# Context attention on one core: four of thirteen tiles squared on GpSimd, an addition in PSUM, and new cyclic orders for four engines

## The chip, the cores and the metric

The program runs on one core of a Trainium2 chip. Its time is the device time of the whole program in microseconds (us), from the launch to the last result in memory. A core has five engines that run their own instruction streams at the same time and wait for each other through semaphores: TensorE (PE in the profile; PEld is its loading of weights), VectorE (DVE), ScalarE (ACT), GpSimd (POOL) and SyncE (SP), which here issues the transfers. Matrix products land in PSUM, everything else lives in SBUF.

## The reference, cut to what matters

The program is a small Perceiver: six stages, of which the first and the fourth are the same kind of attention over a context of 1601 rows for each of 16 batches. The change is in that kind alone.

```python
y_dca, y_main = y[:, -16:, :], y[:, :-16, :]        # 1585 main rows of 256
q  = _ln((x @ Wq + bq).reshape(b, s1, 16, 32), qn_w, qn_b)
kv = concat([y_main @ Wk + bk, y_main @ Wv + bv])   # 512 columns each
k  = _ln(kv[..., :32], kn_w, kn_b)                  # normalised over each head's 32 columns
v  = kv[..., 32:]
ctx = softmax(q @ k.T * 32**-0.5) @ v               # 16 heads, 64 queries per batch
...
x = x + xattn_0(...); x = x + attn_0(...); x = x + ffn_0(...)
x = x + xattn_1(...); x = x + attn_1(...); x = x + ffn_1(...)
```

## The kernel before

`context_attention` is called twice in a run. It works through the 16 batches one after the other, and each batch's 1585 context rows in 13 tiles: twelve of 128 rows and a last one of 49. Values are held as the sum of a float16 part and a float16 rest, so that most products come in three matmuls.

For each tile i of the next batch: PE projects K (`k`, six matmuls of 512 columns into `ps_k`) and V (`v`, into `ps_v`); DVE takes K out of PSUM (`kc`), ACT squares it (`sq`, line 367, with a scale), DVE sums the squares of each head (`rd`, line 460); for each pair of tiles ACT makes a first guess of the inverse root (`r`, lines 373 and 377) and POOL refines it with five small instructions, one Newton step (`nw`, lines 300 to 310); ACT copies the root beside K (`rp`), DVE multiplies (`hat`), ACT and DVE write the float16 part and its rest (`kh`, `kl`), and SP transposes the tile by a transfer. V is split likewise by ACT (`vh`, line 400) and DVE (`vl`, line 482). The context itself is split chunk by chunk by ACT (`yh`) and POOL (`yl`). PE also makes first scores (`m`), of which DVE takes a maximum (line 493), needed to shift the queries (`tb`, `t`, `qs`, `qh`, `ql`; `qm` on POOL).

For the current batch there are 14 units of two tiles, seven for each half of the heads: PE makes the scores (`s`, line 650, into the one PSUM buffer `ps_t`), ACT takes the exponential twice (`e`, line 420 in float32 and 422 in float16), POOL subtracts the two to get the rest (`lo`, line 335), PE multiplies both with V and adds into `ps_o` (`pv`, line 677). After a half, DVE divides (`o`, lines 524 to 531) and the next half may overwrite `ps_o`.

`ps_k`, `ps_v`, `ps_h` and `ps_t` have one buffer each. So `s` of a unit waits until both exponentials of the unit before are done, `k` waits for `kc` of the tile before, and `v` for `vl` of the tile before.

No scheduler decides the order. `ORDER` is a table of four cyclic lists, one each for PE, ACT, DVE and POOL. One trip through a list is called a turn here; in each turn every step of one batch is done once on that engine. A trailing minus shifts a step by one batch back: in turn t, `k2-` is tile 2 of one batch and `s8--` unit 8 of the batch two before it in the pipeline. `batches` walks each list from two turns ahead of the first batch to two behind the last, and leaves out what no batch asks for. Each engine runs its list in order, so an instruction that waits holds up all that stands behind it on that engine. The last batch's `s` and `pv` stand outside the lists. SP has its own fixed loop, which the change doesn't touch.

Of the kernel before, what the change touches and what calls it, by code (L numbers as in the profile page):

```python
# [40 lines left out]
PER = KT // CHUNKS  # L41
WIDEST = MAIN - (CHUNKS - 1) * PER * P + 1
# [10 lines left out]
    PE: k2- pv6-- m7-- s8-- v0- k3- pv7-- s9-- m8-- pv8-- v1- k4- s10-- m9-- v2- pv9-- m10-- s11-- k5- m11--
    PE: v3- s12-- m12-- pv10-- v4- tb-- k6- s13-- v5- k7- pv11-- v6- k8- s0- pv12-- pv13-- k9- v7- s1- m0-
    PE: k10- pv0- s2- m1- v8- k11- m2- s3- pv1-
    ACT: e5-- rp10-- vh11-- sq0- kh10-- e6-- rp11-- r6-- vh12-- yh1- kh11-- e7-- rp12-- sq1- e8-- kh12-- sq2-
    ACT: vh0- r0- sq3- e9-- rp0- vh1- kh0- e10-- vh2- rp1- r1- sq4- e11-- yh2- vh3- kh1- sq5- e12-- rp2- vh4-
    ACT: r2- kh2- qh-- sq6- rp3- vh5- yh3- kh3- e13-- rp4- sq7- vh6- kh4- r3- sq8- rp5- e0- kh5- vh7- rp6- e1-
    ACT: sq9- kh6- e2- vh8- sq10- rp7- yh0 r4- kh7- e3- rp8- vh9- sq11- kh8- e4- rp9- vh10- sq12- r5- kh9-
    DVE: kl10-- m5-- hat11-- kc1- rd0- m6-- kl11-- vl12-- kc2- hat12-- rd1- o0-- m7-- kc3- vl0- m8-- kl12--  # L60
    DVE: rd2- hat0- vl1- rd3- m9-- kl0- kc4- m10-- vl2- hat1- m11-- kc5- vl3- m12-- kl1- t-- rd4- rd5- hat2-
    DVE: qs-- vl4- kc6- kl2- ql-- hat3- vl5- kc7- kl3- rd6- hat4- rd7- kc8- kl4- vl6- hat5- o1-- kc9- kl5-
    DVE: rd8- vl7- hat6- m0- kc10- rd9- m1- kl6- vl8- hat7- rd10- kc11- kl7- m2- hat8- vl9- kc12- kl8- m3-
    DVE: rd11- hat9- vl10- m4- kl9- kc0 hat10- vl11- rd12-
    POOL: lo8-- nw0- lo9-- nw1- lo10-- yl2- lo11-- nw2- lo12-- yl3- qm- lo13-- nw3- lo0- lo1- lo2- nw4- yl0
    POOL: lo3- lo4- nw5- lo5- lo6- nw6- yl1 lo7-
# [3286 lines left out]
```

## Time and profile before

| | us |
|---|---|
| median of 3 runs | 3083.88 (3082.59 to 3091.93) |
| the profiled execution, whole | 3080.41 |
| its span (first to last instruction) | 3078.6 |
| PE busy | 2816.6 (91%) |
| DVE busy | 2570.9 (84%) |
| ACT busy | 2272.8 (74%) |
| POOL busy | 1615.3 (52%) |

Busy time is the union of an engine's instructions. PE's matmuls overlap: one starts before the one ahead of it has left, so for PE the distance between two starts says more than a duration. The two calls of the context attention cover about 104 to 1084 us and 1773 to 2753 us of the span; the rest is self attention, the expert layer and the last layer.

### The profile page before, as it was taken

What the parts mean: (1) busy time and instruction counts of PE and PEld (TensorE: products, weight loads), DVE (VectorE), ACT (ScalarE), POOL (GpSimd) and SP (SyncE); (2) the same over time, 40 slices, a digit from 0 to 9 for tenths busy, and PEclk for the clock granted to TensorE, in tenths of its full rate; (3) what the DMA queues carried; (4) which work ended last, traced back from release to release, by engine and by line L of the source; (5) the groups of instructions that cost most, each with busy time, mean ns of one, the idle gap of its engine ahead of it and who ended that gap; (6) DMA issues with size and microseconds to landing.
All of it is one profiled execution on the core that took longest, in us unless ns stands there. A gap on an engine that the chain in (4) does not pass through costs nothing. (4 is left out here: it accounts for less than half of the span.)

```text
span 3078.6 us, 94131 instructions
## 1 busy us (share of the span) xinstructions
PE 2816.6 (91%) x37417; PEld 1666.0 (54%) x37417; DVE 2570.9 (84%) x4146; ACT 2272.8 (74%) x4155; POOL 1615.3 (52%) x2006
## 2 busy tenths in 40 slices
PE   7689999999999778789996779999999999968889
PEld 3245555555555556577773325555555555545646
DVE  6699999999999656768875679999999999957752
ACT  6479999999999854446664458999999999964431
POOL 1257777777777643212223326777777777752200
PEclk9899999999999889899998899999999999979989
DMA  3345554555554244349895345545555555430020
GB/s 126 95 87 87 97 84 89 94 87 86 94 89 82 56 158 151 133 167 299 301 304 150 104 85 94 90 86 92 90 85 94 88 87 93 73 93 1 1 75 28
DMA packets 542717, 328.93 MB, mean 107 GB/s; under 512 B 459381, under 2 KB 504565, under 8 KB 536522
## 3 DMA queue, kind: packets, MB, share of 16 engines
q1 hardware_dynamic: 534314, 295.63, 43.2%
q0 software_dynamic: 7680, 25.17, 2.8%
q8 instruction: 301, 4.93, 0.7%
q10 hardware_dynamic: 288, 2.10, 0.2%
q14 instruction: 134, 1.10, 0.1%
HBM read 181.86 MB, written 36.09 MB: 71 GB/s over the span
## 5 line engine op out<-in xcount | busy, mean ns | idle before, releaser
L335 POOL TENSOR_TENSOR a_elo<-a_e 128x1024 f16<-128x1024 f32 x428 | 856.5, 2001 | 285.6 <-ACT a_e L422 285.6
L590 PE MATMUL a_ps_k<-l_wk,a_yh 128*128 128x512 f16 (+1 forms) x1664 | 571.3, 384 | 32.5 <-POOL a_yl L317 22.0
L590 PE MATMUL a_ps_v<-l_wv,a_yh 128*128 128x512 f16 (+1 forms) x1664 | 567.8, 382 | 17.9 <-DVE a_v L482 16.9
L493 DVE TENSOR_REDUCE a_mx<-a_ps_m 128x2 f32<-128x1024 f32 x384 | 467.7, 1218 | 20.3 <-PE a_ps_m L616 20.0
L420 ACT ACTIVATE a_e<-a_ps_t 128x1024 f32<-128x1024 f32 x428 | 409.3, 956 | 42.4 <-PE a_ps_t L650 39.9
L422 ACT ACTIVATE a_e<-a_ps_t 128x1024 f16<-128x1024 f32 x428 | 410.5, 959 | 0.0
L650 PE MATMUL a_ps_t<-a_qb,a_kk 64*128 64x128 f16 (+1 forms) x9672 | 351.0, 219 | 8.9 <-ACT a_e L422 8.3
L650 PEld LDWEIGHTS a_ps_t<-a_qb,a_kk 64*128 64x128 f16 (+1 forms) x9672 | 281.6, 96 | 122.8 <-issue 90.7
L590 PE MATMUL a_ps_k<-l_wk,a_yl 128*128 128x512 f16 (+1 forms) x832 | 318.4, 383 | 0.0
L452 DVE SCALAR_TENSOR_TENSOR a_kc<-a_ps_k,l_bk 128x512 f32<-128x512 f32 (+1 forms) x416 | 283.2, 681 | 41.4 <-PE a_ps_k L590 40.2
L590 PE MATMUL a_ps_v<-l_wv,a_yl 128*128 128x512 f16 (+1 forms) x832 | 315.9, 380 | 0.0
L400 ACT ACTIVATE a_v<-a_ps_v 128x512 f16<-128x512 f32 (+1 forms) x416 | 255.4, 614 | 73.0 <-PE a_ps_v L590 60.3
L590 PEld LDWEIGHTS a_ps_k<-l_wk,a_yh 128*128 128x128 f16 (+1 forms) x1664 | 164.1, 99 | 255.0 <-issue 63.1
L677 PEld LDWEIGHTS a_ps_o<-a_v,a_e 128*64 128x64 f16 (+1 forms) x6480 | 230.0, 113 | 131.5 <-issue 98.8
L482 DVE SCALAR_TENSOR_TENSOR a_v<-a_ps_v,a_v 128x512 f16<-128x512 f32 (+1 forms) x416 | 284.3, 683 | 15.7 <-ACT a_v L400 11.2
L392 ACT ACTIVATE a_khl<-a_ps_h,a_one 128x512 f16<-128x512 f32 (+1 forms) x416 | 284.1, 683 | 16.4 <-DVE a_ps_h L467 15.9
L467 DVE TENSOR_TENSOR a_ps_h<-a_kc,a_ps_h 128x512 f32<-128x512 f32 (+1 forms) x416 | 285.8, 687 | 9.6 <-ACT a_ps_h L384 4.7
L590 PEld LDWEIGHTS a_ps_v<-l_wv,a_yh 128*128 128x128 f16 (+1 forms) x1664 | 163.1, 98 | 239.8 <-issue 43.3
L677 PE MATMUL a_ps_o<-a_v,a_e 128*64 128x65 f16 (+1 forms) x6480 | 273.4, 201 | 20.6 <-POOL a_elo L335 14.0
L475 DVE SCALAR_TENSOR_TENSOR a_khl<-a_ps_h,a_khl 128x512 f16<-128x512 f32 (+1 forms) x416 | 283.0, 680 | 1.7 <-ACT a_khl L392 1.7
L367 ACT ACTIVATE a_sq<-a_kc 128x512 f32<-128x512 f32 (+1 forms) x416 | 260.2, 625 | 26.0 <-DVE a_kc L452 23.4
L460 DVE TENSOR_REDUCE a_var<-a_sq 128x16 f32<-128x512 f32 (+1 forms) x416 | 277.8, 674 | 0.0
(415 smaller groups left out, 5283.9 us busy)
## 6 DMA issues: line engine op xcount, KB each, us to landing
l_land<-in_ctx SPq DMA_DIRECT2D x96, 384.0 KB, 3.9
l_ob<-in_m_w SPq DMA_DIRECT2D x32, 1024.0 KB, 8.0
f_w<-in_m_w SPq DMA_DIRECT2D x32, 512.0 KB, 4.8
...
```

What stands on the lines that cost most here:

```text
L335: pool.tensor_tensor(rest[0:r, :, 0:w], full[0:r, :, 0:w], high[0:r, :, 0:w], ALU.subtract)\
L392: act.activation(khl[0:r, n % 2, 0, :], ps_h[0:r, :], ACT.Identity, bias=one[0:r, 0:1])\
L420: act.activation(full[0:r, :, 0:w], src[0:r, :, 0:w], ACT.Exp)
L422: act.activation(high[0:r, :, 0:w], src[0:r, :, 0:w], ACT.Exp).then_inc(e_done, 1)
L452: dve.scalar_tensor_tensor(out=kc[0:r, kc_slot(at, i), :], in0=ps_k[0:r, :], scalar=1.0 / WSCALE, in1=bk[0:r, :], op0=ALU.mult, op1=ALU.ad ...
L467: dve.tensor_tensor(ps_h[0:r, :].rearrange("p (h d) -> p h d", d=HD), kc[0:r, kc_slot(at, i), :].rearrange("p (h d) -> p h d", d=HD), ps_h ...
L475: dve.scalar_tensor_tensor(out=khl[0:r, n % 2, 1, :], in0=ps_h[0:r, :], scalar=1.0, in1=khl[0:r, n % 2, 0, :], op0=ALU.add, op1=ALU.subtract)\
L482: dve.scalar_tensor_tensor(out=v[0:r, at.nbp, i, :, VLO:OW], in0=ps_v[0:r, :].rearrange("p (h d) -> p h d", d=HD), scalar=1.0 / WSCALE, in ...
L493: dve.tensor_reduce(mx[:, g, :, c], ps_m[:, :, :], AX.X, ALU.max).then_inc(mx_done, 1)
L590: m = pe.matmul(out[0:r, :], part[:, n % 2, c, cols], w[:, wpart, c, :], start=(c == 0 and a == 0), stop=(c == KC - 1 and a == 2))
L650: t = pe.matmul(dst[0:rows(i), r, col:col + P], kk[d, at.bp, kpart + g, k], qb[d, at.bp, g, qpart, :, :].rearrange("p a q -> p (a q)"), st ...
L677: t = pe.matmul(ps_o[q, a * OW:a * OW + w], part[k, r, col + 64 * par:col + 64 * par + 64], v[k, at.bp, i, 2 * pair + par, 0:w], start=fir ...
```

## The change

Four things change, all inside `context_attention`:

1. The squares of tiles 2, 5, 8 and 11 are taken by POOL, as a product of `kc` with itself, and no longer by ACT. DVE's sum waits on a new semaphore for them.
2. The square has no scale any more; the factor 1/32 is applied where the variance is read, in ACT's logarithm and in POOL's first Newton instruction, which adds the small constant in the same instruction (a product and a sum with two constants in place of a sum of two tensors).
3. In `out`, the sum of the two value parts is written back into `ps_o` in PSUM and no longer into `ob` in SBUF; the last product reads it there.
4. All four lists are in a new order. Their first step is another one too, so that the shifts (the minus signs) differ.

```diff
--- before.py
+++ after.py
@@ -39,6 +39,7 @@
 VLO = 33
 CHUNKS = 4
 PER = KT // CHUNKS
+POOL_SQUARES = (2, 5, 8, 11)
 WIDEST = MAIN - (CHUNKS - 1) * PER * P + 1
 WSCALE = 32.0
 LN_EPS, HEAD_EPS = 1e-5, 1e-6
@@ -49,21 +50,22 @@
 
 
 ORDER = """
-    PE: pv2-- v9-- k12-- s4-- m3-- v10-- pv3-- s5-- m4-- k0- v11-- pv4-- m5-- s6-- k1- v12-- s7-- pv5-- m6--
...
+    PE: m6-- s8-- k2- pv7-- s9-- m7-- k3- v1- pv8-- m8-- s10-- v2- m9-- k4- pv9-- s11-- m10-- v3- k5- m11--
...
 """
 
 
@@ -140,7 +142,7 @@
         q_in = [sem("q_in0"), sem("q_in1")]
         yh_done, yl_done = sem("yh_done"), sem("yl_done")
         k_done, v_done = sem("k_done"), sem("v_done")
-        kc_done, sq_done, red_done = sem("kc_done"), sem("sq_done"), sem("red_done")
+        kc_done, sq_done, red_done, psq_done = sem("kc_done"), sem("sq_done"), sem("red_done"), sem("psq_done")
         ln_done, r0_done, hat_done = sem("ln_done"), sem("r0_done"), sem("hat_done")
         newton = [sem(f"newton{j}") for j in range(5)]
         kh_done, kl_done, rp_done = sem("kh_done"), sem("kl_done"), sem("rp_done")
@@ -182,6 +184,10 @@
                 n = len(range(k, tiles, 2))
                 if n:
                     eng.wait_ge(turned[k], 16 * n)
+
+        def squared(tiles):
+            b, i = divmod(tiles, KT)
+            return b * len(POOL_SQUARES) + sum(k < i for k in POOL_SQUARES)
 
         def tiles_of(j):
             tp = j % TPAIRS
@@ -297,8 +303,7 @@
                     n, u, nt, r = at.nb * TPAIRS + p, (at.nbp * TPAIRS + p) % 2, len(tiles_of(p)), rows(2 * p)
                     v2, r2, a2, b2 = (t[0:r, u, 0:nt, :] for t in (var, r0, na, nb_))
                     pool.wait_ge(r0_done, n + 1)
-                    pool.tensor_tensor(a2, v2, eps[0:r, 0:nt * H].rearrange("p (t h) -> p t h", h=H), ALU.add)\
-                        .then_inc(newton[0], 1)
+                    pool.tensor_scalar(a2, v2, 1.0 / HD, HEAD_EPS, ALU.mult, ALU.add).then_inc(newton[0], 1)
                     pool.tensor_tensor(b2, r2, r2, ALU.mult).then_inc(newton[1], 1)
                     pool.wait_ge(newton[0], n + 1)
                     pool.wait_ge(newton[1], n + 1)
@@ -317,6 +322,13 @@
                     pool.tensor_tensor(yl[:, n % 2, :, 0:hi - lo], y[:, :, lo:hi], yh[:, n % 2, :, 0:hi - lo],
                                        ALU.subtract).then_inc(yl_done, 1)
 
+                def square(at, i):
+                    n, t, r = at.nb * KT + i, tile_par(at.nbp, i), rows(i)
+                    pool.wait_ge(kc_done, n + 1)
+                    need(pool, red_done, n - 1)
+                    full = kc[0:r, kc_slot(at, i), :]
+                    pool.tensor_tensor(sq[0:r, t, :], full, full, ALU.mult).then_inc(psq_done, 1)
+
                 def q_first(at):
 
                     pool.wait_ge(q_in[at.nbp], at.load)
@@ -340,6 +352,8 @@
                         newton_step(at, i)
                     elif kind == "yl":
                         y_low(at, i)
+                    elif kind == "sq" and i in POOL_SQUARES:
+                        square(at, i)
                     elif kind == "qm":
                         q_first(at)
                     elif kind == "lo" and (at.b < B - 1 or i % 2 == 0):
@@ -364,13 +378,14 @@
                     n, t, r = at.nb * KT + i, tile_par(at.nbp, i), rows(i)
                     act.wait_ge(kc_done, n + 1)
                     need(act, red_done, n - 1)
-                    act.activation(sq[0:r, t, :], kc[0:r, kc_slot(at, i), :], ACT.Square, scale=SCALE).then_inc(sq_done, 1)
+                    act.activation(sq[0:r, t, :], kc[0:r, kc_slot(at, i), :], ACT.Square).then_inc(sq_done, 1)
 
                 def guess(at, p):
 
                     n, u, nt, r = at.nb * TPAIRS + p, (at.nbp * TPAIRS + p) % 2, len(tiles_of(p)), rows(2 * p)
                     act.wait_ge(red_done, at.nb * KT + 2 * p + nt)
-                    act.activation(lnv[0:r, u, 0:nt, :], var[0:r, u, 0:nt, :], ACT.Ln, bias=eps[0:r, 0:1])\
+                    act.activation(lnv[0:r, u, 0:nt, :], var[0:r, u, 0:nt, :], ACT.Ln, scale=1.0 / HD,
+                                   bias=eps[0:r, 0:1])\
                         .then_inc(ln_done, 1)
                     need(act, newton[4], n - 1)
                     act.wait_ge(ln_done, n + 1)
@@ -424,7 +439,7 @@
                 def step(kind, i, at):
                     if kind == "yh":
                         y_high(at, i)
-                    elif kind == "sq":
+                    elif kind == "sq" and i not in POOL_SQUARES:
                         square(at, i)
                     elif kind == "r":
                         guess(at, i)
@@ -454,7 +469,10 @@
 
                 def variance(at, i):
                     n, t, r = at.nb * KT + i, tile_par(at.nbp, i), rows(i)
-                    dve.wait_ge(sq_done, n + 1)
+                    if i in POOL_SQUARES:
+                        dve.wait_ge(psq_done, squared(n + 1))
+                    else:
+                        dve.wait_ge(sq_done, n + 1 - squared(n + 1))
                     p = i // 2
                     need(dve, newton[4], at.nb * TPAIRS + p - 1)
                     dve.tensor_reduce(var[0:r, (at.nbp * TPAIRS + p) % 2, i % 2, :], sq[0:r, t, :].rearrange("p (h d) -> p h d", d=HD), AX.X, ALU.add)\
@@ -525,10 +543,10 @@
                     osum = ob[:, at.b, half * P:half * P + P].rearrange("p (a d) -> p a d", d=HD)
                     dve.tensor_copy(osum, o3[:, :, VLO:OW]).then_inc(os_done, 1)
                     dve.wait_ge(os_done, 2 * n + 1)
-                    dve.tensor_tensor(osum, o3[:, :, 0:HD], osum, ALU.add).then_inc(os_done, 1)
+                    dve.tensor_tensor(o3[:, :, 0:HD], o3[:, :, 0:HD], osum, ALU.add).then_inc(os_done, 1)
                     dve.wait_ge(rl_done, n + 1)
                     dve.wait_ge(os_done, 2 * n + 2)
-                    dve.tensor_tensor(osum, osum, rl[:, half, :].unsqueeze(2).broadcast_to([P, 4, HD]), ALU.mult)\
+                    dve.tensor_tensor(osum, o3[:, :, 0:HD], rl[:, half, :].unsqueeze(2).broadcast_to([P, 4, HD]), ALU.mult)\
                        .then_inc(o_done, 1)
 
                 def low(at, j):
```

The first place is PE's list around the units 7 to 9. `a_ps_t` are scores (128x128 x24 is a whole unit), `a_ps_m` first scores, `a_ps_k` and `a_ps_v` projections, `a_ps_o` the values. Before, from `s8` to the start of `pv7` (batches in the middle of the first call):

```order
L616 MATMUL a_ps_m<-a_kk,a_qm 128x512 x2
L650 MATMUL a_ps_t<-a_qb,a_kk 128x128 x24
L590 MATMUL a_ps_v<-l_wv,a_yh 128x512
L590 MATMUL a_ps_v<-l_wv,a_yl 128x512
L590 MATMUL a_ps_v<-l_wv,a_yh 128x512 x2
L590 MATMUL a_ps_v<-l_wv,a_yl 128x512
L590 MATMUL a_ps_v<-l_wv,a_yh 128x512
L590 MATMUL a_ps_k<-l_wk,a_yh 128x512
L590 MATMUL a_ps_k<-l_wk,a_yl 128x512
```

And after:

```order
L634 MATMUL a_ps_m<-a_kk,a_qm 128x512 x2
L668 MATMUL a_ps_t<-a_qb,a_kk 128x128 x24
L608 MATMUL a_ps_k<-l_wk,a_yh 128x512
L608 MATMUL a_ps_k<-l_wk,a_yl 128x512
L608 MATMUL a_ps_k<-l_wk,a_yh 128x512 x2
L608 MATMUL a_ps_k<-l_wk,a_yl 128x512
L608 MATMUL a_ps_k<-l_wk,a_yh 128x512
L695 MATMUL a_ps_o<-a_v,a_e 64x65 x2
```

Between `s8` and `pv7` (and so `s9`, which stands behind `pv7` in both) there were two projections, and now there is one.

The second place is ACT's list around the same units: `a_v` of 49 rows is `vh12`, `a_yh` is `yh1`, `a_khl` is `kh`, `a_e` are the exponentials, `a_ps_h` is `rp`. Before:

```order
L373 ACTIVATE a_lnv<-a_var,a_eps 49x16
L377 ACTIVATE a_r<-a_lnv 49x16
L400 ACTIVATE a_v<-a_ps_v 49x16x32
L361 ACTIVATE a_yh<-l_land 128x2x384
L392 ACTIVATE a_khl<-a_ps_h,a_one 128x512
L420 ACTIVATE a_e<-a_ps_t 128x1024
L422 ACTIVATE a_e<-a_ps_t 128x1024
L384 ACTIVATE a_ps_h<-a_rstd 49x16
L367 ACTIVATE a_sq<-a_kc 128x512
L420 ACTIVATE a_e<-a_ps_t 128x1024
L422 ACTIVATE a_e<-a_ps_t 128x1024
```

And after:

```order
L415 ACTIVATE a_v<-a_ps_v 49x16x32
L407 ACTIVATE a_khl<-a_ps_h,a_one 128x512
L387 ACTIVATE a_lnv<-a_var,a_eps 49x16
L392 ACTIVATE a_r<-a_lnv 49x16
L375 ACTIVATE a_yh<-l_land 128x2x384
L399 ACTIVATE a_ps_h<-a_rstd 128x16
L435 ACTIVATE a_e<-a_ps_t 128x1024
L437 ACTIVATE a_e<-a_ps_t 128x1024
L381 ACTIVATE a_sq<-a_kc 128x512
L407 ACTIVATE a_khl<-a_ps_h,a_one 128x512
L435 ACTIVATE a_e<-a_ps_t 128x1024
L437 ACTIVATE a_e<-a_ps_t 128x1024
```

The wait for `v12` stands farther ahead of `e7` (the first `a_e` pair), and a square and a `kh` now stand between `e7` and `e8`.

The third place is POOL's list from `lo7` on: `a_elo` is `lo`, the five small ones are `nw0`, `a_yl` is `yl2`. Before:

```order
L335 TENSOR_TENSOR a_elo<-a_e 128x1024 x2
L300 TENSOR_TENSOR a_na<-a_var,a_eps 128x32
L302 TENSOR_TENSOR a_nb<-a_r 128x32
L305 TENSOR_TENSOR a_na<-a_na,a_nb 128x32
L307 TENSOR_SCALAR a_na<-a_na 128x32
L310 TENSOR_TENSOR a_rstd<-a_r,a_na 128x32
L335 TENSOR_TENSOR a_elo<-a_e 128x1024
```

And after:

```order
L347 TENSOR_TENSOR a_elo<-a_e 128x1024 x2
L306 TENSOR_SCALAR a_na<-a_var 128x32
L307 TENSOR_TENSOR a_nb<-a_r 128x32
L310 TENSOR_TENSOR a_na<-a_na,a_nb 128x32
L312 TENSOR_SCALAR a_na<-a_na 128x32
L315 TENSOR_TENSOR a_rstd<-a_r,a_na 128x32
L330 TENSOR_TENSOR a_sq<-a_kc 128x512
L347 TENSOR_TENSOR a_elo<-a_e 128x1024
L322 TENSOR_TENSOR a_yl<-l_land,a_yh 128x2x384
```

A square (tile 2) now stands between `nw0` and `lo9`; the other three stand behind `lo10`, `nw3` and `nw4`.

## Rows read from the trace of the kernel before

**Rows 1.** Stretches: us, busy us (instructions) of PE, PEld, DVE, ACT, POOL, clock, DMA, GB/s.
```profile
355.40:935.40 580.00, 578.45 (x9482) 317.87 (x9481) 566.93 (x901) 543.11 (x1001) 431.59 (x541) 1.00 0.54 89
104.00:182.00 78.00, 60.55 (x254) 22.11 (x254) 64.94 (x98) 40.76 (x91) 21.24 (x53) 0.93 0.39 80
```

**Rows 2.** Timeline of DVE, one row per turn: start us, us, line, operation.
```profile
355.39 0.18 DVE L503 TENSOR_REDUCE a_mxx<-a_mx 128x8 f32<-128x32 f32 x1
...
935.41 0.18 DVE L503 TENSOR_REDUCE a_mxx<-a_mx 128x8 f32<-128x32 f32 x1
```

**Rows 3.** Timeline of PE, units 7 to 9 of one turn.
```profile
681.41 0.84 PE L650 MATMUL a_ps_t<-a_qb,a_kk 64*128 64x128 f16 x24
...
682.80 0.39 PE L616 MATMUL a_ps_m<-a_kk,a_qm 64*128 64x512 f16 x2
683.12 0.39 PE L590 MATMUL a_ps_k<-l_wk,a_yh 128*128 128x512 f16 x1
...
684.52 0.22 PE L677 MATMUL a_ps_o<-a_v,a_e 49*64 49x65 f16 x2
...
684.88 0.39 PE L616 MATMUL a_ps_m<-a_kk,a_qm 64*128 64x512 f16 x2
685.28 0.84 PE L650 MATMUL a_ps_t<-a_qb,a_kk 64*128 64x128 f16 x24
686.06 0.39 PE L590 MATMUL a_ps_v<-l_wv,a_yh 128*128 128x512 f16 x1
...
687.37 0.38 PE L590 MATMUL a_ps_k<-l_wk,a_yh 128*128 128x512 f16 x1
...
688.75 0.22 PE L677 MATMUL a_ps_o<-a_v,a_e 128*64 128x65 f16 x2
...
689.37 0.84 PE L650 MATMUL a_ps_t<-a_qb,a_kk 64*128 64x128 f16 x24
690.05 0.38 PE L616 MATMUL a_ps_m<-a_kk,a_qm 64*128 64x512 f16 x2
690.56 0.22 PE L677 MATMUL a_ps_o<-a_v,a_e 128*64 128x65 f16 x2
```

**Rows 4.** Timeline of ACT beside them; in brackets the idle time before, and its releaser.
```profile
681.51 0.61 ACT L400 ACTIVATE a_v<-a_ps_v 49x512 f16<-49x512 f32 x1 [0.74 <-PE a_ps_v L590]
...
682.74 0.67 ACT L392 ACTIVATE a_khl<-a_ps_h,a_one 128x512 f16<-128x512 f32 x1
683.31 1.01 ACT L420 ACTIVATE a_e<-a_ps_t 128x1024 f32<-128x1024 f32 x1
684.22 1.01 ACT L422 ACTIVATE a_e<-a_ps_t 128x1024 f16<-128x1024 f32 x1
...
686.17 1.02 ACT L420 ACTIVATE a_e<-a_ps_t 128x1024 f32<-128x1024 f32 x1 [0.28 <-PE a_ps_t L650]
```

**Rows 5.** Timeline of POOL beside them.
```profile
685.31 2.13 POOL L335 TENSOR_TENSOR a_elo<-a_e 128x1024 f16<-128x1024 f32 x1 [0.80 <-ACT a_e L422]
688.18 2.23 POOL L335 TENSOR_TENSOR a_elo<-a_e 128x1024 f16<-128x1024 f32 x1 [0.74 <-ACT a_e L422]
690.75 0.25 POOL L300 TENSOR_TENSOR a_na<-a_var,a_eps 128x32 f32<-128x32 f32 x1 [0.33 <-ACT a_r L377]
...
691.98 0.25 POOL L310 TENSOR_TENSOR a_rstd<-a_r,a_na 128x32 f32<-128x32 f32 x1
```

**Rows 6.** Timeline of DVE beside them: the output's last instruction.
```profile
688.13 0.29 DVE L531 TENSOR_TENSOR l_ob<-l_ob,a_rl 128x128 f32<-128x128 f32 x1
```

**Rows 7.** Groups by form, POOL, whole span: busy us, mean ns, idle before.
```profile
L324 POOL TENSOR_TENSOR a_qm<-a_q,parity_mask 128x512 f16<-128x512 f32 x32 | 33.2, 1037 | 0.0
L1638 POOL TENSOR_TENSOR s_ox<-l_ob,l_land 128x512 f32<-128x512 f32 x4 | 7.1, 1770 | 0.1
```

**Rows 8.** Groups by line in the ten turns: busy us, mean ns, idle before.
```profile
L373 ACT ACTIVATE a_lnv<-a_var,a_eps 128x32 f32<-128x32 f32 (+1 forms) x70 | 22.3, 319 | 0.0
L377 ACT ACTIVATE a_r<-a_lnv 128x32 f32<-128x32 f32 (+1 forms) x70 | 15.9, 227 | 6.4
```

More of the change, by code:

```diff
@@ L51 @@
 ORDER = """
-    PE: pv2-- v9-- k12-- s4-- m3-- v10-- pv3-- s5-- m4-- k0- v11-- pv4-- m5-- s6-- k1- v12-- s7-- pv5-- m6--
[L53 to L66, printed above, removed]
+    PE: m6-- s8-- k2- pv7-- s9-- m7-- k3- v1- pv8-- m8-- s10-- v2- m9-- k4- pv9-- s11-- m10-- v3- k5- m11--
@@ new lines @@
+    PE: v4- pv10-- s12-- m12-- v5- k6- s13-- tb-- v6- k7- pv11-- pv12-- v7- k8- s0- pv13-- m0- v8- s1- m1- k9-
+    PE: v9- pv0- s2- k10- pv1- m2- s3- k11- v10- pv2- m3- s4- k12- v11- pv3- s5- k0 pv4- m4- s6- v12- k1 pv5-
+    PE: s7- m5- v0 pv6-
+    ACT: vh8-- kh5-- e1-- rp6-- yh0- sq9-- kh6-- e2-- rp7-- vh9-- r4-- kh7-- e3-- rp8-- sq10-- vh10-- kh8--
+    ACT: e4-- rp9-- r5-- vh11-- kh9-- e5-- rp10-- sq12-- sq0- e6-- vh12-- kh10-- r6-- yh1- rp11-- e7-- sq1-
+    ACT: kh11-- e8-- rp12-- vh0- e9-- r0- kh12-- vh1- rp0- e10-- kh0- vh2- sq3- yh2- sq4- rp1- vh3- e11-- kh1-
@@ new lines @@
+    ACT: vh4- r1- e12-- rp2- vh5- kh2- yh3- rp3- r2- sq6- vh6- kh3- qh-- rp4- e13-- sq7- kh4- vh7- r3- rp5-
+    ACT: e0-
+    DVE: kc2- hat12-- vl0- rd1- m7-- kc3- kl12-- vl1- m8-- hat0- rd2- m9-- vl2- kc4- kl0- m10-- hat1- vl3-
+    DVE: rd3- kc5- m11-- vl4- rd4- m12-- kl1- rd5- hat2- t-- vl5- kl2- kc6- qs-- hat3- rd6- vl6- kl3- kc7-
+    DVE: hat4- ql-- rd7- kl4- vl7- kc8- m0- hat5- o1-- vl8- kl5- kc9- rd8- hat6- m1- rd9- kl6- kc10- hat7-
+    DVE: vl9- m2- kl7- kc11- hat8- rd10- vl10- rd11- kl8- kc12- hat9- m3- kl9- vl11- kc0 hat10- m4- rd12- rd0
@@ L67 @@
+    DVE: vl12- kl10- kc1 m5- hat11- o0- m6- kl11-
+    POOL: yl0- lo2-- nw4-- sq11-- lo3-- lo4-- nw5-- lo5-- lo6-- nw6-- yl1- lo7-- lo8-- nw0- sq2- lo9-- yl2-
+    POOL: lo10-- sq5- nw1- lo11-- lo12-- nw2- yl3- qm- lo13-- nw3- sq8- lo0- lo1-
 """
```

## The prediction

> **What bounds the kernel now.** I read the stretches first, then the time of one turn, then PE's timeline with those of ACT, POOL and DVE beside it. In ten turns of the first call PE is busy 578.45 of 580 us, DVE 566.93, ACT 543.11 and POOL 431.59, at a granted clock of 1.00 [rows 1]. A busy PE isn't yet a PE without waits, since each matmul's end is modelled and lies over the next one's start. So I go by starts. The marker of a turn comes at 355.39 and, ten turns on, at 935.41: 58.00 us a turn [rows 2].
>
> In PE's timeline nearly every block takes the same time wherever it stands [rows 3]. From its first start to the next block's: a projection followed by a projection 1.31 (686.06 to 687.37), a projection followed by something else 1.38 to 1.40, a unit of scores 0.68 before first scores (689.37 to 690.05) and 0.78 before a projection, values 0.62, first scores before a projection 0.32, the tail's values 0.36. So a block costs about 0.09 more where the next has another form of matmul (full rows, 64 rows, 64 columns, or one of these with the tail's 49), the difference between 1.31 and 1.40. That is PE's price for a switch. Two blocks take longer than this ledger. First scores `m7` last 0.40 before `s8` (684.88 to 685.28) where no form changes, so 0.23 (0.32 less a switch) would do: 0.17 of wait. First scores `m8` last 0.51 before `pv8` (690.05 to 690.56) in place of 0.32: 0.19 of wait.
>
> Each has a visible cause. `s8` starts 0.05 after the second exponential of unit 7 ends (684.22 + 1.01 = 685.23), and that pair is late because ACT sat 0.74 before `vh12`, which stands ahead of it [rows 4]. `pv8` starts 0.15 after POOL's `lo8` ends (688.18 + 2.23 = 690.41) [rows 5]. So the bound is PE's own work at 99% of the turn, plus some tenths of waiting; nothing can win more than those tenths.
>
> **The change, part by part.** *Four squares leave ACT.* ACT is busy 54.3 of 58 us a turn; four instructions of some 0.57, like `kh` (682.74 to 683.31, also 512 columns), make 2.3 less. PE waits for ACT only at `s8`, so by itself this is worth at most the 0.17 there. *They come to POOL.* POOL is busy 43.2 of 58 a turn. No row shows a float32 product of a tile with itself. The nearest below is `qm`, 128x512 in 1.04; the longest of this size is 1.77 [rows 7]. That is 4.1 to 7.1 a turn, 47 to 50 of 58, so POOL doesn't become the bound by its sum. I take 1.04, because `lo` too costs 2.13 for 1024 columns, thus about 1.07 for 512. The Trainium skill, "GPSIMD Engine Reference", section "Performance versus the Vector engine", gives 4497 ns for a float32 sum of two tensors of 2048 columns; an estimate from it is 1.12 for 512, which would leave the sum as it is. *The scale and the small constant* stay in instructions that are there anyway: 0, hidden on ACT and POOL.
>
> *The sum in PSUM.* DVE's last output instruction has both inputs in SBUF before, and one of them in PSUM after. It starts at 688.13 [rows 6], `lo8` at 688.18, and this `lo8` takes 2.23 where the one before took 2.13 [rows 5]. So 0.10 of the 0.19 at `pv8` is this collision; it comes back every turn, as the order does. After the change it can't. "SBUF — State Buffer", in its diagram's rules on the shared port pair, says in the Trainium skill that a DVE instruction with two SBUF inputs and a GpSimd one that reads SBUF exclude each other, the later one waiting; by that rule the 0.10 goes wherever the four lists put it, and the trace agrees with the size of a part of a short instruction. The instruction itself may cost a few hundredths more or less in PSUM; twice a turn, hidden on DVE unless DVE is the bound.
>
> *The new orders.* PE's blocks are the same. Counting switches of form around the cycle, the tail's 49 rows as forms of their own, I find 50 before and 51 after: +0.09 a turn. The two waits above go (0.36): `vh12` now stands four instructions ahead of `e7`, and `s8` to `pv8` is longer. New ones come. Scores of the next unit need, from start to start, 0.89 (685.28 to 686.17) + 1.93 (683.31 to 685.23) + 0.05 = 2.87. After the change `s8` to `s9` holds only 0.78 + 1.40 + 0.62 = 2.80: 0.07 short. Further, `s7` to `s8` is 0.68 + 0.32 + 1.40 + 0.36 + 0.23 = 2.99, so on a clock that is 0 at `s8`, `e7` runs from -2.10 to -0.17, then a square and a `kh` of about 0.57 or a little less each are queued ahead of `e8`, which starts at 0.95 and not at 0.89: 0.06. So `s9` waits 0.13. `s0` to `s1` holds 0.78 + 0.36 + 0.32 + 1.40 = 2.86: 0.01. `s7` to `pv7` holds 2.99 + 0.78 + 1.40 = 5.17 and needs 0.89 + 1.93 + 0.07 + 2.13 + 0.15 = 5.17: 0. I take 0.15. What is queued behind a late `s9` on PE is all the rest of the turn, so each tenth counts in full.
>
> *Run-in and end.* The first call's run-in takes 78 us with DVE busy 64.94 [rows 1], so DVE and latencies set it. After the change one more tile's projections stand ahead of the first marker; DVE does about four more instructions there and PE some 2.7 us that it then needn't do later. I take 0, with 3 us to either side for both calls.
>
> The sum: a turn goes from 58.00 to 58.00 - 0.36 + 0.09 + 0.15 = 57.88. Each call has about 14 full turns, so 28 x -0.12 = -3.4 us. The profiled execution took 3080.41; it becomes 3077.0. The median of the runs shown stands 3.5 above the profiled one, so the median to expect is 3080.5, in round figures 3081. That is 0.1% less. About 0.3%, 9 us, is what a measurement of this kernel can tell from no change.
>
> **The rivals.** *PE at its floor.* Any other wait that hides in the 58.00 goes too, and the new 0.15 doesn't show because ACT has 2.3 us more room. Then a turn is 58.00 - 0.36 - 0.08 (one more wait of the kind, of which I have no place) + 0.09 = 57.65, and 28 x -0.35 = -9.8: 3074. For it speaks that three of four engines gain or keep room; against it that 2.80 is less than 2.87 whatever ACT does.
>
> *POOL's queue, slower.* The place is `nw0`, the square of tile 2, `lo9`, and behind it `pv9`. On the clock above, `s9` starts at 2.93, `e9` at 3.82 and ends at 5.75, the guess (0.32 + 0.23) [rows 8] at 6.30, `nw0` takes 1.48 (690.75 to 691.98 + 0.25) and ends at 7.86. A square of 1.04 ends at 8.95, `lo9` at 11.08, and `pv9` could start at 11.23. PE's own blocks bring it there at 2.93 + 8.46 = 11.39 (units, projections and switches as above). The margin is 0.16: a square over 1.20 makes PE wait. At 1.77 it is 0.57 a turn, +16 us in 28, thus 3097. For it: the rows of POOL spread from 1.04 to 1.77. Against it: the 1.77 is 4 instances outside these calls.
>
> *DVE or V's copies late, slower.* DVE is busy 98% of a turn, and the new lists put `vh3` ahead of `e11` on ACT; `e11`, `kh1`, `vh4`, `vl4` then stand in a row before `v5` with about a tenth to spare. If DVE comes half an instruction late there and at one like place, a turn takes 0.3 more than forecast plus what hangs on it: +5 to +12 us, about 3092. That the lists do the opposite of their numbers is no case here: they are followed as written.
>
> **How the numbers follow.** The forecast, waits exchanged for waits of the same size: 0.50, at 3081. PE at its floor: 0.20, at 3074. POOL's queue: 0.13, up to 3097. V's copies or DVE: 0.17, near 3092. The floor is on the side of faster by over 0.3%, with a run-in that helps; the last two are slower by over 0.3% but for a part of the last. So faster 0.21, same 0.53, slower 0.26. The range reaches from the floor with its 3 us of run-in, 3070, to POOL's end, 3098; the forecast's own is 3075 to 3087.
>
> **What would show it.** The marker's distance is the turn: 57.88 by the forecast, 57.65 at the floor, 58.2 and more if slower. `s8` to `s9` starts should be about 2.93 apart, and PE's idle or stretched places should be there, not at `m7` and `m8`. No `lo` should take 2.23 beside the output. The squares on POOL should take 1.04 to 1.2, and POOL be busy about 47 a turn, ACT about 52. A turn under 57.6 or over 58.3, or a run-in that moves by over 2 us, would make the working wrong.

## The result and the profile after

The changed kernel takes 3090.47 us (median of 22 runs, 3082.86 to 3095.9), the kernel before 3083.95 beside it (22 runs, 3074.71 to 3091.93). The ratio is 1.0019 [1.0011, 1.0027]: slower by 6.5 us. That is less than the 0.3% named in the prediction, but clear of no change, and on the other side of it than the 3081 that was forecast.

The profiled execution took 3091.25 us, its span 3089.4. First the page's busy times (us, share of the span, instructions):

```profile
PE 2820.5 (91%) x37417; PEld 1675.1 (54%) x37417; DVE 2567.7 (83%) x4146; ACT 2223.9 (72%) x4027; POOL 1743.9 (56%) x2134
```

Three stretches of the changed kernel: the run-in and ten turns, as in [rows 1], and the 37 us behind the first call's last marker. Columns are those of [rows 1].

```profile
107.50:187.30 79.80, 62.84 (x266) 23.14 (x266) 67.47 (x100) 39.41 (x87) 27.19 (x58) 0.95 0.38 75
360.90:940.30 579.40, 577.95 (x9481) 320.07 (x9480) 565.55 (x901) 528.45 (x960) 471.72 (x581) 1.00 0.49 90
1050.70:1087.70 37.00, 26.13 (x804) 23.20 (x804) 11.98 (x20) 27.40 (x34) 16.77 (x9) 0.77 0.01 3
```

In ten turns ACT went from 543.11 to 528.45 and POOL from 431.59 to 471.72: the work moved as foreseen. The markers, which answer to [rows 2]:

```profile
360.92 0.18 DVE L521 TENSOR_REDUCE a_mxx<-a_mx 128x8 f32<-128x32 f32 x1
...
940.36 0.18 DVE L521 TENSOR_REDUCE a_mxx<-a_mx 128x8 f32<-128x32 f32 x1
...
1050.75 0.19 DVE L521 TENSOR_REDUCE a_mxx<-a_mx 128x8 f32<-128x32 f32 x1
```

These ten turns take (940.36 - 360.92) / 10 = 57.94 us each, where 58.00 stood before and 57.88 was forecast. So the turn got a little shorter, and the kernel longer. I cut each call at five places: its first `k`, its first marker, the marker 14 turns on, the last marker, and the end of its last values. Each figure is the mean over both calls of two traces, the second from the runs *again_before* and *again_after*:

| us per call | run-in | 14 turns | last turn | end | sum |
|---|---|---|---|---|---|
| before | 77.7 | 811.5 | 54.0 | 36.2 | 979.5 |
| changed | 79.8 | 812.0 | 51.7 | 38.3 | 981.9 |

The run-in's 2.1 comes back in the last turn (2.3), the end is 2.1 longer, and the 14 turns, which should have given 1.7 a call, give nothing. The calls thus hold about 5 of the 6.5 us. What lies outside the calls is the same code in both, and differs by up to 3 us from one trace to the next of one kernel (the part between the calls took 689.0 and 692.0 in the two traces of before). So a single span can't show a difference of this size; the stages and the medians must.

### The profile page after: what moved, and what is told of

Read it like the earlier page. It is cut to its first block and busy times, and to the rows that moved or that the text cites. A ratio compares the mean times of both kernels' runs of the same rounds, so it can differ in the third digit from the quotient of the medians.

```text
span 3089.4 us, 94131 instructions
## 1 busy us (share of the span) xinstructions
PE 2820.5 (91%) x37417; PEld 1675.1 (54%) x37417; DVE 2567.7 (83%) x4146; ACT 2223.9 (72%) x4027; POOL 1743.9 (56%) x2134
## 5 line engine op out<-in xcount | busy, mean ns | idle before, releaser
L695 PE MATMUL a_ps_o<-a_v,a_elo 128*64 128x33 f16 (+1 forms) x6480 | 263.4, 185 | 0.0
```

The lines of the kernel that those rows point to most:

```text
L695: t = pe.matmul(ps_o[q, a * OW:a * OW + w], part[k, r, col + 64 * par:col + 64 * par + 64], v[k, at.bp, i, 2 * pair + par, 0:w], start=fir ...
```

## Why the end is longer

PE's timeline around the last marker of the first call, in the changed kernel (start us, us, engine, line; in brackets the idle time before and its releaser):

```profile
1049.73 0.37 PE L634 MATMUL a_ps_m<-a_kk,a_qm 64*128 64x49 f16 x8
1051.97 0.84 PE L668 MATMUL a_ps_t<-a_qb,a_kk 64*49 64x128 f16 x12 [1.87 <-ACT a_e L437]
1052.73 1.08 PE L644 MATMUL a_ps_m<-fall,a_mxx 128*32 128x64 f32 x32
```

The same place in the kernel before:

```profile
1047.60 0.18 DVE L503 TENSOR_REDUCE a_mxx<-a_mx 128x8 f32<-128x32 f32 x1
1047.84 0.65 PE L626 MATMUL a_ps_m<-fall,a_mxx 128*32 128x64 f32 x32 [0.27 <-DVE a_mxx L503]
1048.89 0.52 PE L650 MATMUL a_ps_t<-a_qb,a_kk 64*49 64x128 f16 x12 [0.40 <-ACT a_e L422]
```

`tb` works on the marker's result, and what follows in the call hangs on it. Before, it stood ahead of `s13` and came 0.24 us after the marker (1047.84 - 1047.60). Now `s13` stands ahead of it. In a full turn that makes no wait: the projections `v5` and `k6` stand before `s13` and give ACT time, and `k6` to `s13` takes the usual 1.39. In the last turn there are no projections: `s13` waits 1.87 for the exponentials of unit 12, and `tb`, queued behind it, comes 1.98 after the marker (1052.73 - 1050.75). This is 1.74 later for everything that follows in the first call. In the second call `s13` waits 1.74, and `tb` comes 1.55 after the marker, so 1.31 later than before.

Is the clock a rival? In the first call's end it was granted at 0.77 in the changed kernel and at 0.86 in the kernel before:

```profile
1047.60:1084.60 37.00, 24.76 (x852) 21.88 (x852) 13.57 (x22) 27.65 (x34) 17.90 (x10) 0.86 0.01 4
```

In the second call it was the other way round, 0.86 and 0.82, and the changed kernel's end is still the longer one (37.3 against 36.2). What share of the end runs at the lower of the clock's two levels differs between calls and executions of one kernel.

## What the turns lost

In the kernel before, the turns are even: the median of a call's 14 is 57.98, and one turn in four calls is more than 0.1 above it. In the changed kernel the median is 57.91 to 57.94, which is the ordinary turn, but three to six turns in each call take about 0.1 to 0.4 more. Together these single waits cost 1.0 us a call (0.1 before), as much as the shorter ordinary turn gives. In about half of them PE's first scores wait for the transfer that transposes a tile, as here in the second call:

```profile
2252.20 0.39 PE L634 MATMUL a_ps_m<-a_kk,a_qm 64*128 64x512 f16 x2 [0.31 <-DMA a_kk<-a_khl]
```

The largest is in the first turn of the first call. There PE waits 0.64 for such a transfer in the first trace of the changed kernel and 1.89 in *again_after*, where the matmuls then take 0.61 in place of 0.39 (the clock was granted at 0.68 in the 5 us that follow). The two rows, *again_after* second:

```profile
195.78 0.39 PE L634 MATMUL a_ps_m<-a_kk,a_qm 64*128 64x512 f16 x2 [0.64 <-DMA a_kk<-a_khl]
...
195.19 0.61 PE L634 MATMUL a_ps_m<-a_kk,a_qm 64*128 64x512 f16 x2 [1.89 <-DMA a_kk<-a_khl]
```

That turn takes 57.5 in the one and 60.3 in the other. Six traces have the changed lists, with one or two steps moved at most, and the four squares on POOL and the sum in PSUM. Three of them have this turn long (*again_after*, *qm_later*, *m7_first*), and none of the six traces with the lists of before. Without that turn the 14 turns take 811.3. What makes these transfers late was not tested.

The ordinary turn itself loses time mainly at one place. POOL's timeline, the changed kernel, from `nw1` to `lo13` of one turn:

```profile
705.86 0.22 POOL L306 TENSOR_SCALAR a_na<-a_var 128x32 f32<-128x32 f32 x1 [0.59 <-ACT a_r L392]
...
707.39 4.22 POOL L347 TENSOR_TENSOR a_elo<-a_e 128x1024 f16<-128x1024 f32 x2
711.69 0.22 POOL L306 TENSOR_SCALAR a_na<-a_var 128x32 f32<-128x32 f32 x1
...
713.22 1.78 POOL L322 TENSOR_TENSOR a_yl<-l_land,a_yh 128x866 f16<-128x866 f32 x1
714.95 1.04 POOL L336 TENSOR_TENSOR a_qm<-a_q,parity_mask 128x512 f16<-128x512 f32 x1
715.95 1.15 POOL L347 TENSOR_TENSOR a_elo<-a_e 49x512 f16<-49x512 f32 x1
```

and PE beside it:

```profile
716.29 0.84 PE L668 MATMUL a_ps_t<-a_qb,a_kk 64*128 64x128 f16 x24
717.25 0.22 PE L695 MATMUL a_ps_o<-a_v,a_e 49*64 49x65 f16 x2
```

From `nw1` at 705.86 POOL runs seven pieces without a gap: `nw1`, `lo11`, `lo12`, `nw2`, `yl3`, `qm`, `lo13`, until 717.10. `s0` to `pv13` is then 0.96 to 0.98 from start to start; with no wait it would be 0.77, as `s0` to `pv12` is before. So `pv13` waits 0.20 each turn for `lo13`. The prediction had no such place: I had followed POOL's queue only to `pv9` and `pv7`.

`m7` and `m8` no longer wait, as foreseen. `s8` to `s9` holds 690.09 - 687.23 = 2.86 where 2.77 to 2.80 would do without a wait, so it waits 0.06 to 0.09; 0.13 was forecast:

```profile
687.23 0.83 PE L668 MATMUL a_ps_t<-a_qb,a_kk 64*128 64x128 f16 x24
687.99 0.39 PE L608 MATMUL a_ps_k<-l_wk,a_yh 128*128 128x512 f16 x1
...
689.42 0.22 PE L695 MATMUL a_ps_o<-a_v,a_e 128*64 128x65 f16 x2
690.09 0.84 PE L668 MATMUL a_ps_t<-a_qb,a_kk 64*128 64x128 f16 x24
690.77 0.38 PE L634 MATMUL a_ps_m<-a_kk,a_qm 64*128 64x512 f16 x2
```

One more wait went that I hadn't seen. In the kernel before `s13` lasts 0.53 ahead of `v5`, where `s6`, the other unit of one tile, lasts 0.45 ahead of `k1`. `v5` starts 0.05 after DVE has taken `vl4` out of `ps_v` (705.68 + 0.68 = 706.36), so it waits 0.08 each turn:

```profile
705.68 0.68 DVE L482 SCALAR_TENSOR_TENSOR a_v<-a_ps_v,a_v 128x512 f16<-128x512 f32 x1
705.88 0.52 PE L650 MATMUL a_ps_t<-a_qb,a_kk 64*49 64x128 f16 x12
...
706.41 0.10 PEld L590 LDWEIGHTS a_ps_v<-l_wv,a_yh 128*128 128x128 f16 x1 [0.18 <-DVE a_v L482]
```

In the changed lists `s13` takes 0.45. With this the ordinary turn adds up: 57.98 - 0.36 (`m7`, `m8`) - 0.08 (`v5`) + 0.09 (a switch more) + 0.09 (`s9`) + 0.20 (`pv13`) = 57.92, and 57.91 was measured.

## The experiments

My theory on seeing the traces: two places cost the kernel its gain, `tb` behind `s13` in the last turn (3.4 us) and `qm` ahead of `lo13` on POOL (about 5). The rivals: POOL's squares themselves, the PSUM sum, or chance. Timings come in three batches, in which before took 3084.22 (35 runs), 3084.19 (23) and 3083.14 (29).

**The measurement itself.** *again_before* is the kernel before once more, beside itself.

> The kernel before once more, for the length of its stages in a second profile. Theory E (the end of each call): call by call the run-in is 77.5 us, 14 turns 811.5, the last turn 54, the end 36.2, as in the first profile, within 0.5; then differences of 2 us between kernels in these stages are real. Theory N (the unchanged parts differ by chance): what lies ahead of the first call, between the two and behind the second (104.5, 689.0 and 325.9 us in the first profile) moves by 1 to 3 us from one profile to the next. Rival to N: these parts come out as before within 0.5, and the changed kernel's 107.5, 691.1 and 327.7 are its own.

3083.86, ratio 1.0002 [0.9992, 1.0011]. Two like kernels come out within 0.4 us here; the interval of one such comparison reaches about 3 to 4 us to either side, here and below.

*again_after* is the changed kernel once more.

> The changed kernel once more. Theory E: run-in 79.7, 14 turns 811.0 to 811.5, last turn 52.3, end 37 to 39.5 in each call, 981 to 983 us in all against 979.5 of before. Theory N: 107.5, 691.1 and 327.7 us ahead, between and behind come back closer to 104.5, 689.0 and 325.9 in this profile; rival: they stay within 0.5 of the first profile of this kernel. Ratio of times to before 1.001 to 1.003.

3089.97, 1.0023 [1.0011, 1.0036]. The loss is real, and chance is out.

**The two places, each mended alone.** *tb_first* is the changed kernel, in the last turn of a call `tb` ahead of `s13`:

```
 elif kind == "tb":
     shift_rows(at)
+    if at.nb == B - 1:
+        scores(At(B - 2), UNITS - 1)
 ...
-    scores(at, i)
+    if at.b < B - 2 or i < UNITS - 1:
+        scores(at, i)
```

> The changed kernel, but in the last turn of each call PE makes the shift rows (tb) before the scores of unit 13, and not behind them. Theory E: in the last turn the scores wait 1.9 us for the exponentials of unit 12 and hold up tb and with it the last batch; with tb first it starts 0.3 us after its marker and not 2.0, and the end of each call shrinks by 1.7 us, 3.4 for the program. Rival (the end is longer because of the clock or of the last batch itself): the marker-to-end time stays at 37 to 39.

3085.47, 1.0007 [0.9994, 1.0019], 4.5 us less than *again_after*. Its trace has `tb` 0.24 after the marker again in both calls, and an end of 36.1 and 36.8 us in the two calls:

```profile
1046.81 0.19 DVE L521 TENSOR_REDUCE a_mxx<-a_mx 128x8 f32<-128x32 f32 x1
1047.05 0.65 PE L644 MATMUL a_ps_m<-fall,a_mxx 128*32 128x64 f32 x32 [0.88 <-DVE a_mxx L521]
1047.91 0.52 PE L668 MATMUL a_ps_t<-a_qb,a_kk 64*49 64x128 f16 x12 [0.21 <-ACT a_e L437]
```

*tb_behind* does the reverse to the kernel before: in the last turn `tb` stands behind `s13`.

```
 elif kind == "tb":
-    shift_rows(at)
+    if at.nb < B - 1:
+        shift_rows(at)
 ...
 scores(at, i)
+if at.b == B - 2 and i == UNITS - 1:
+    shift_rows(At(B - 2))
```

> The kernel before, but in the last turn of each call the shift rows (tb) stand behind unit 13's scores, as in the changed kernel. Theory E from its other side: tb comes 1.5 to 2 us later after the marker, the end of each call is 38 to 39 us and not 36.2, the program 3.5 to 4.5 us slower, near 3088. Rival (the end's length hangs on the new lists elsewhere): 36.2 and 3084 stay.

3088.55, 1.0021 [1.0009, 1.0034]: 5.4 us more than before, from this edit alone. In its trace `s13` waits 1.32 and `tb` comes 1.74 after the marker:

```profile
1050.78 0.18 DVE L503 TENSOR_REDUCE a_mxx<-a_mx 128x8 f32<-128x32 f32 x1
1052.07 0.52 PE L650 MATMUL a_ps_t<-a_qb,a_kk 64*49 64x128 f16 x12 [1.32 <-ACT a_e L422]
1052.52 0.65 PE L626 MATMUL a_ps_m<-fall,a_mxx 128*32 128x64 f32 x32
```

The end is 37.3 and 38.5 us in it, 1.7 over before's on average. So the place of `tb` in the last turn is shown from both sides. Its price is known best from the stages. Over all 14 traces the end is 35.9 to 38.1 us where `tb` comes at once (16 calls, mean 36.7, `tb` 0.25 after the marker) and 37.3 to 39.4 where it comes behind `s13` (12 calls, mean 38.3, `tb` 1.82 after it): `tb` comes 1.6 later and the end is 1.6 longer, 3.2 for the two calls. The medians' 4.5 and 5.4 agree with that within their intervals. Nor is it the clock: `tb` takes 0.65 in this run's first call and 1.08 in its second, and so it does in the kernel before, whose end is 36.2 both times.

*qm_later* is the changed kernel with one step moved in POOL's list:

```
-... nw2- yl3- qm- lo13-- nw3- sq8- ...
+... nw2- yl3- lo13-- qm- nw3- sq8- ...
```

> The changed kernel, but on POOL the queries' mask product (qm, 1.0 us) stands behind lo13 and not ahead of it. Theory Q (POOL's queue from nw1 to lo13 makes pv13 wait 0.20 us a turn): lo13 comes 1 us earlier, the 0.20 goes, a turn is 57.75 to 57.8 and not 57.93, 14 turns 808.5, 5 us less for the program. Rival: the wait turns up elsewhere (first scores m0 then wait for qm, or the next queued unit), and a turn stays at 57.9.

3086.08, 1.0006 [0.9997, 1.0015], 3.9 less than *again_after* (5 was expected; the interval holds both). Its POOL and PE:

```profile
716.55 1.16 POOL L347 TENSOR_TENSOR a_elo<-a_e 49x512 f16<-49x512 f32 x1
717.66 1.04 POOL L336 TENSOR_TENSOR a_qm<-a_q,parity_mask 128x512 f16<-128x512 f32 x1
...
717.85 0.84 PE L668 MATMUL a_ps_t<-a_qb,a_kk 64*128 64x128 f16 x24
718.63 0.22 PE L695 MATMUL a_ps_o<-a_v,a_e 49*64 49x65 f16 x2
```

`lo13` ends at 717.71, before `s0` is through, and `s0` to `pv13` is 0.78. The ordinary turn takes 57.73, 0.18 less.

*both* has both edits.

> The changed kernel with tb ahead of unit 13's scores in the last turn, and with qm behind lo13 on POOL. Theories E and Q together: the two gains (4.5 and 3.9 us when made alone) add up, as they lie in different stretches, a turn is 57.80, the end of a call 36 to 37, the program 3081 to 3082, 8.4 under the changed kernel and 2 to 3 under the one before. Rival (one eats the other's gain): 3085.

3082.04, 0.9993 [0.9982, 1.0003]: 8 us under the changed kernel, and 4.5 + 3.9 = 8.4, so they add up. 14 turns take 809.1 and 809.4. With the two places mended the kernel stands near the 3081 of the forecast. Part of that is luck: the wait at `v5` that went (0.08 a turn) was not in the forecast's sum, and a forecast made with it would have stood lower. And 3082.04 can't be told from the kernel before, since the interval holds 1.

**The parts of the change alone.** *psum_sum* is the kernel before with the sum in PSUM and nothing else:

```
-dve.tensor_tensor(osum, o3[:, :, 0:HD], osum, ALU.add)
+dve.tensor_tensor(o3[:, :, 0:HD], o3[:, :, 0:HD], osum, ALU.add)
 ...
-dve.tensor_tensor(osum, osum, rl..., ALU.mult)
+dve.tensor_tensor(osum, o3[:, :, 0:HD], rl..., ALU.mult)
```

> The kernel before with one part of the change alone: the output's two value sums are added in place in PSUM. Theory P (the collision of the output's last instruction with lo8 on POOL costs PE 0.10 of the 0.19 at pv8 each turn): lo8 takes 2.13 and not 2.23, m8 lasts 0.41 to 0.42 before pv8 and not 0.51, a turn 57.90, 14 turns 810.1, and the program is 2.8 us shorter. Rival (the collision is hidden, or the instruction is dearer in PSUM): a turn stays at 57.97.

3081.72, 0.9986 [0.9973, 0.9998]. Its DVE, POOL and PE at the place of [rows 5] and [rows 6]:

```profile
688.00 0.29 DVE L531 TENSOR_TENSOR l_ob<-a_ps_o,a_rl 128x128 f32<-128x128 f32 x1
688.05 2.14 POOL L335 TENSOR_TENSOR a_elo<-a_e 128x1024 f16<-128x1024 f32 x1 [0.74 <-ACT a_e L422]
...
689.92 0.38 PE L616 MATMUL a_ps_m<-a_kk,a_qm 64*128 64x512 f16 x2
690.34 0.22 PE L677 MATMUL a_ps_o<-a_v,a_e 128*64 128x65 f16 x2
```

The two start as close as before, and `lo8` takes 2.14, not 2.23; `m8` to `pv8` is 0.42, not 0.51. Four calls' 14 turns in this trace and in that of the repeat take 810.0 to 810.4, where before took 811.5: 1.3 us a call, 2.6 a kernel. In the kernel before 28 of POOL's 372 instructions of this size take 2.23 or 2.24, one in each turn; here none does. *psum_again* is the same kernel again, since the interval nearly reached 1:

> The kernel before with the sum in PSUM alone, once more, as the other candidate for a version that beats both: 14 turns 810.3 us, the program 2.5 to 2.8 us under the kernel before, ratio 0.999.

3080.4, 0.9987 [0.9973, 1.0]. Both say 2.5 to 2.7 us less, at the edge of what one timing shows, and the traces say the same at the place foreseen. Together with *both* this is the fastest version; the two can't be told apart (0.3 us in one batch).

*sbuf_sum* is the changed kernel with those two lines taken back.

> The changed kernel with the output's sum in SBUF again, the new lists kept. In the new lists the output of a call's first half runs on DVE while POOL is inside lo7. Theory P: DVE's last output instruction, second to come and with two inputs in SBUF, waits until lo7 ends; it takes 1 to 1.7 us and not 0.29, DVE (98% busy) can't make up for all of it, a turn grows by 0.3 to 0.9 us, the program by 8 to 25 us. Rival (the edit is worth the 0.10 of before at most): the time stays within 3 us of the changed kernel.

3147.62, 1.0216 [1.0194, 1.0239]: 57 us over the changed kernel, where I expected 8 to 25: the mechanism was right, the price too low. Its POOL and DVE:

```profile
703.71 2.13 POOL L347 TENSOR_TENSOR a_elo<-a_e 128x1024 f16<-128x1024 f32 x1
704.06 0.29 DVE L546 TENSOR_TENSOR l_ob<-a_ps_o,l_ob 128x128 f32<-128x128 f32 x1
704.46 1.53 DVE L549 TENSOR_TENSOR l_ob<-l_ob,a_rl 128x128 f32<-128x128 f32 x1
705.91 1.21 DVE L511 TENSOR_REDUCE a_mx<-a_ps_m 128x2 f32<-128x1024 f32 x1
```

Here it is DVE that comes second. Its instruction with one input in PSUM (L546) runs inside `lo7` at its usual 0.29; the one with both in SBUF (L549) takes 1.53 and ends at 705.99, 0.15 after `lo7` ends at 705.84. DVE is held for 1.24 us, and with it the maximum behind it. That happens in both outputs of nearly every turn: 58 of the 64 such instructions take 1.28 to 1.84 us, and each of them ends 0.14 or 0.15 after the `lo` beside it; the six that meet no work of POOL take 0.29. `k3`, `v2` and `v9` then wait on DVE's copies, 0.72, 0.40 and 1.02 more than in the changed kernel, and a turn takes 60.07. Collisions of these two instructions cost 0.10 a turn in the old order (one, POOL second) and 2.16 in the new (two, DVE second). The Trainium skill, "SBUF — State Buffer", section "SBUF: two separate sides", says of the shared port pair that whichever starts first keeps the pair for its whole instruction and the other is blocked; the trace agrees, in that DVE ends 0.15 behind POOL whatever its own length. The other way round it agrees less well: in the kernel before `lo8` starts with 0.24 of DVE's instruction to come, and takes only 0.10 longer.

*pool_squares* is the changed kernel with the orders of before; the squares stand in POOL's list behind `lo8`, `yl2`, `nw3` and `nw4`.

```
-    POOL: yl0- lo2-- nw4-- sq11-- lo3-- ... lo8-- nw0- sq2- lo9-- ...
+    POOL: lo8-- sq2- nw0- lo9-- nw1- lo10-- yl2- sq5- lo11-- nw2- lo12-- yl3- qm- lo13-- nw3- sq8- lo0-
+    POOL: lo1- lo2- nw4- sq11- yl0 lo3- lo4- nw5- lo5- lo6- nw6- yl1 lo7-
```

> The whole change but for the new orders: before's four lists, with the four squares taken out of ACT's and set into POOL's behind lo8, yl2, nw3 and nw4. Theory S (PE waits for ACT at s8 only, because vh12 comes late, so ACT's 2.1 us less per turn are worth nothing, and POOL's queue from lo11 to lo13 grows by a square): s8's wait stays at 0.17, pv13 now waits 0.1 to 0.2, a turn is 57.95 to 58.1, the program 0 to 4 us slower than with the sum alone. Rival (room on ACT is worth something): a turn is 57.8 or less.

3106.14, 1.0064 [1.0049, 1.0079]: 24 us over *psum_sum*, where 0 to 4 was expected. A turn takes 58.63 where 57.89 stood. Its POOL and PE at the costliest place:

```profile
676.31 1.04 POOL L329 TENSOR_TENSOR a_sq<-a_kc 128x512 f32<-128x512 f32 x1
677.30 1.59 POOL L321 TENSOR_TENSOR a_yl<-l_land,a_yh 128x768 f16<-128x768 f32 x1
678.85 2.13 POOL L346 TENSOR_TENSOR a_elo<-a_e 128x1024 f16<-128x1024 f32 x1
...
681.13 0.22 PE L694 MATMUL a_ps_o<-a_v,a_e 128*64 128x65 f16 x2 [0.55 <-POOL a_elo L346]
```

Behind `nw4` stand the square, `yl0` and then `lo3`, so `pv3` waits. That place takes 0.62 a turn more and `pv12` with `pv13` 0.13 more. `m7` still takes 0.40 ahead of `s8`, so ACT's relief gained nothing there. Other places for the squares were not tried. POOL is busy 465 of 579 us in ten turns and still sets the time.

*act_squares* is the changed kernel with its new orders, but all squares on ACT: `sq2` behind `vh1`, `sq5` behind `r1`, `sq8` behind `vh8`, `sq11` behind `kh8`.

> The changed kernel with all thirteen squares on ACT again: the four stand behind vh1, r1, vh8 and kh8 in ACT's new list, POOL's list loses them, the rest of the change stays. Theory O (the orders make the turn, the squares do not; the 0.20 at pv13 comes from POOL's chain that starts when ACT has made r1): a turn stays at 57.9 to 58.0, and pv13 still waits 0.15 to 0.3. Rival (POOL's squares cost PE the 0.20): pv13's wait goes and a turn is 57.75.

3101.01, 1.0051 [1.0035, 1.0066], 11 us over the changed kernel; 14 turns take 817.2 and 815.8, the ordinary turn 58.26 to 58.30 (57.9 to 58.0 was expected). `pv13` waits 0.19 a turn here too, with no square on POOL, so the square isn't what makes `lo13` late. The new loss is 0.25 a turn at `pv7`, and 0.11 at `s3`, which waits for unit 2's exponentials. ACT and POOL ahead of `pv7`:

```profile
688.46 0.22 ACT L390 ACTIVATE a_r<-a_lnv 49x16 f32<-49x16 f32 x1
...
688.76 0.20 POOL L306 TENSOR_SCALAR a_na<-a_var 49x16 f32<-49x16 f32 x1 [0.42 <-ACT a_r L390]
...
690.15 1.59 POOL L322 TENSOR_TENSOR a_yl<-l_land,a_yh 128x768 f16<-128x768 f32 x1
691.70 2.12 POOL L347 TENSOR_TENSOR a_elo<-a_e 128x1024 f16<-128x1024 f32 x1
```

With more on ACT the guess `r6` comes later, `nw6` waits for it, and `yl1`, `lo7` and `pv7` stand behind without a gap. ACT's relief is worth 0.35 a turn in these lists, more than half of it through POOL's queue and next to none through `s8`; the four squares stood where I put them, and other places were not tried.

**The wait at `s9`.** *m7_first* is *both* with one pair exchanged in PE's list, `pv7-- s9-- m7-- k3-` to `pv7-- m7-- s9-- k3-`, which gives ACT 0.3 us more before `s9`.

> The changed kernel with tb first in the last turn, qm behind lo13, and m7 ahead of s9 on PE. Theory W (s8 to s9 has 2.80 us and needs 2.87 to 2.90): with m7 between them the window is 3.03, the 0.09 of wait at k2/pv7 before s9 goes, a turn is 57.72, the program 2.5 us under the 3082 without this swap, 3079.5. Rival: the wait moves to k3 or to pv8 and a turn stays at 57.81.

3086.52, 1.0015 [1.0001, 1.0028]. The expectation (3079.5) failed and its rival held. The wait at `s9` shrinks, but `vl1` comes 0.17 later on DVE and `v2` 0.21 later behind `s10`: the ordinary turn takes 57.90, where *both* has 57.73. In the view of waits, over ten turns, PE's wait for DVE's V copies rises from 5.1 to 8.2 us. So the small wait at `s9` was not worth removing in this way: it comes back as a wait for DVE.

## Why the prediction was wrong

The measured 3090.47 lies within the whole range (3070 to 3098), above the forecast's own (3075 to 3087) and on the other side of the kernel before. It came there by a term that no rival had, the end, and by one that the rival on POOL's queue had in kind only.

**The stage that was taken as nothing.** The step that failed is "*Run-in and end* ... I take 0, with 3 us to either side for both calls". For the run-in the reasoning held: 2.1 us more there, 2.3 less in the last turn, though 2.1 is over the 2 us that the prediction itself had named as a sign against it. For the end I had named nothing that hides the new order, although the lists are followed in the last turn as well, with the steps of a turn that doesn't exist left out. There `tb` behind `s13` makes each end 1.6 us longer, 3.2 in all; by the medians 4.5 us (*tb_first*) and 5.4 (*tb_behind*), each to within about 4.

**A queue followed to the wrong place.** The second step that failed is "The sum: a turn goes from 58.00 to ... 57.88": it missed 0.20 at `pv13`, 5 us a kernel. Two smaller errors go the other way: the wait at `s9` took 0.06 to 0.09 instead of 0.13, and the wait at `v5` (0.08) went. That is the size of the term in the rival "PE at its floor" for which I had no place; the trace of the kernel before had shown it. So the ordinary turn, 57.91, came near the 57.88 by errors that nearly cancel.

**Turns taken as all alike.** "28 x -0.12 = -3.4" took each full turn to gain the same. The ordinary turn gained 0.07, and the single late turns took it back: 14 turns last 811.3 where 811.5 stood, and 2.8 more when the first turn is long. So the full turns gave none of the 3.4, and the two ends cost 3.2 (all traces) to 4.3 (the table). The rest of the 6.5 is less than the intervals leave open.

The rival on POOL's queue had the right kind of place, a late `lo` behind a row of POOL's work, but the wrong one and the wrong cause: it asked for a square over 1.20, and 128 squares took 1035 to 1042 ns, median 1039. The 1.04 taken was right. The rival on V's copies came only in single turns: in one turn of the first call `v2` comes 0.28 late behind DVE's copy.

**The parts that held.** The collision's removal was put at 0.10 a turn, 2.8 us; alone it gave 0.10 a turn and 2.5 to 2.7 us. The waits at `m7` and `m8` are gone. POOL's busy time was put at 47 a turn, ACT's at 52; 47.2 and 52.8 were measured. One switch of form more was right too. The time with both places mended is 3082.0, near the 3081 forecast, in part by luck.

**Two statements that were too wide.** That the relief of ACT is worth at most 0.17 because "PE waits for ACT only at `s8`" fell with *act_squares*: in the new lists it is worth 0.35. In the old ones it was worth nothing at `s8` (*pool_squares*). And the collision was priced at 0.10 "wherever the four lists put it": that holds for its removal, but what it would cost depends on the order: 0.10 a turn where POOL came second once, 2.16 where DVE came second twice.

**What stays open.** The two edits take 8 us away from a kernel that was 6.5 slower; what is left, 2 us under the kernel before, is not clear of nothing. What the squares, the orders and the PSUM sum each contribute to *both*, which is no faster than the PSUM sum alone, isn't settled, nor why single transposes come late in the new order and what the long first turn, in three traces of six, does to the median.
